# Fourth quarter of a pass: the order in which SyncE issues V's reads and writes and the read of projected rows

## The reference

```python
def _L0_ffn_ref(x, Wq, Wk, Wv, Ws, Wd, Wo):      # 16 heads, 8 experts, 2 chosen
    q = jnp.einsum('btc,hdc->bhtd', x, Wq)
    k = jnp.einsum('btc,hdc->bhtd', x, Wk)
    gate_v = jnp.einsum('btc,hec->bthe', x, Ws)
    w, sel = jax.lax.top_k(gate_v, K)
    mix_v = jnp.einsum('bthk,bthke->bthe', sigmoid(w), one_hot(sel))
    proj_v = jnp.einsum('btc,edc->bted', x, Wv)
    v = jnp.einsum('bthe,bted->bhtd', mix_v, proj_v)
    probs = softmax(einsum('bhid,bhjd->bhij', q * scale, k))
    attn = jnp.einsum('bhij,bhjd->bihd', probs, v)
    mask_o = ...                                  # top 2 of x @ Wd
    return jnp.einsum('bthe,bthd,efd->bthf', mask_o, attn, Wo).sum(axis=2)
...
x = x + 0.5 * _L0_ffn_ref(_layernorm(x), ...)
x = x + _L0_attn_ref(_layernorm(x), ...)
x = x + 0.5 * _L0_ffn_ref(_layernorm(x), ...)
```

## Time and profile before

| | |
|---|---|
| timed, median of 3 | 2392.2 us |
| the profiled execution's own time | 2388.17 us |
| its span, first to last instruction | 2386.4 us |
| TensorE clock granted | 0.998 of full speed |
| TensorE busy (matmul) | 2293.9 us, 96% |
| VectorE, ScalarE, GpSimd busy | 86%, 82%, 49% |
| DMA | 388 MB, mean 163 GB/s, queues 55% busy |

### The profile page before, as it was taken

The page is one execution under the profiler, slowest core; times in us unless marked ns, Lnnn a source line. Parts: engine busy times, 40 slices in busy tenths (PEclk is TensorE's granted clock), DMA queues, the critical chain, the costliest instruction groups (busy, mean ns, idle before and its releaser), DMA issues.

```text
span 2386.4 us, 120494 instructions
## 1 busy us (share of the span) xinstructions
PE 2293.9 (96%) x49920; PEld 2148.7 (90%) x49920; DVE 2060.7 (86%) x3755; ACT 1950.4 (82%) x6053; POOL 1161.0 (49%) x1190
## 2 busy tenths in 40 slices
PE   3999999999999999999999999999999999999997
PEld 3899898999999999999999999999999999999897
DVE  5888888989889898888989888888888888898884
ACT  2888787888888888888888888888888888888885
POOL 3445555455455454454454454454454454554431
PEclk9999999999999999999999999999999999999999
DMA  4555555655555555556556556556556555556553
GB/s 122 160 171 154 147 161 149 171 164 169 163 164 170 167 168 168 161 164 174 162 166 173 162 164 178 163 164 173 166 165 175 162 168 165 169 163 172 161 166 103
DMA packets 660701, 388.23 MB, mean 163 GB/s; under 512 B 232512, under 2 KB 585664, under 8 KB 660160
## 3 DMA queue, kind: packets, MB, share of 16 engines
q1 hardware_dynamic: 659728, 379.67, 55.0%
q10 hardware_dynamic: 432, 0.85, 0.1%
HBM read 191.64 MB, written 188.74 MB: 159 GB/s over the span
## 4 chain that ended last, share of the span: by engine, by line
PE 86%; ACT 6%; issue 4%; DVE 2%; POOL 1%; DMA 0%; SPq 0%; ACTq 0%; DVEq 0%; POOLq 0%
PE psT L477 19%; PE psS L432 15%; PE psT L494 8%; PE psT L496 6%; PE psT L495 6%; PE psS L524 6%; PE psT L524 6%; PE psT L445 6%; PE psT L489 5%; PE psT L459 5%; ACT PB L812 5%; ACT PJ L853 1%; DVE NMAX L693 1%; PE psT L603 1%; PE psT L530 1%
## 5 line engine op out<-in xcount | busy, mean ns | idle before, releaser
L812 ACT ACTIVATE PB<-psS,NMAX 128x256 f32<-128x256 f32 x2048 | 943.5, 488 | 101.4 <-DVE NMAX L693 101.4
L477 PE MATMUL psT<-V,PT 128*64 128x64 f32 x16384 | 544.3, 224 | 22.9 <-issue 22.2
L477 PEld LDWEIGHTS psT<-V,PT 128*64 128x64 f32 x16384 | 505.3, 138 | 51.7 <-issue 26.5
L812 ACT ACTIVATION_READ_ACCUMULATOR PB<-psS,NMAX 128x1 f32 x2048 | 452.8, 221 | 0.0
L761 DVE TENSOR_TENSOR QK<-psT,QK 128x512 fp32r<-128x512 f32 x512 | 349.0, 688 | 119.0 <-ACT QK L820 112.4
L432 PE MATMUL psS<-QK 64*128 64x256 f32 x6144 | 442.8, 288 | 3.1 <-DVE PT L765 2.6
L820 ACT ACTIVATE QK<-psT 128x512 fp32r<-128x512 f32 x512 | 307.3, 602 | 164.8 <-PE psT L496 141.0
L432 PEld LDWEIGHTS psS<-QK 64*128 64x128 f32 x6144 | 393.5, 187 | 8.3 <-issue 4.7
L693 DVE TENSOR_REDUCE NMAX<-psS 128x2 f32<-128x512 f32 x512 | 329.6, 685 | 51.5 <-PE psS L432 48.1
L927 POOL TENSOR_TENSOR BT<-MT,diagv 128x1024 f32<-128x1024 f32 x128 | 304.5, 2379 | 110.4 <-DMA MT<-MIXd 106.3
L933 POOL TENSOR_TENSOR MB<-MASKT,diago 128x1024 f32<-128x1024 f32 x128 | 250.2, 1956 | 144.3 <-DVE GM L770 116.4
(11 more groups left out here) (121 smaller groups left out, 4777.9 us busy)
## 6 DMA issues: line engine op xcount, KB each, us to landing
Vd<-VM SPq DMA_DIRECT2D x512, 128.0 KB, 2.3
V<-Vd SPq DMA_DIRECT2D x512, 128.0 KB, 3.1
AOd<-AO SPq DMA_DIRECT2D x256, 256.0 KB, 2.7
AR<-AOd SPq DMA_DIRECT2D x256, 256.0 KB, 4.1
PJd<-PJ SPq DMA_DIRECT2D x64, 512.0 KB, 2.8
PR<-PJd SPq DMA_DIRECT2D x256, 128.0 KB, 2.5
MIXd<-MIX SPq DMA_DIRECT2D x64, 128.0 KB, 2.3
MT<-MIXd SPq DMA_DIRECT2D x64, 128.0 KB, 3.3
```

The costliest lines, as they stand in the source:

```text
L477: last = eng.matmul(M[64 * u:64 * u + 64, (t * NT + it) * DH:(t * NT + it + 1) * DH], PT[:, t, jt, cols], V[:, pm % 2, 4 * r + t, jt, :], ...
L812: eng.activation(PB[:, ab, j, it, :], psS[:, ab, j, it, :], ACT.Exp, bias=NMAX[:, ab, j, it:it + 1], accum_out=SUM[:, p % 2, it, 4 * r + t ...
```

## The change

In the fourth quarter (r = 3) SP's order was: read V's first half, read PR, write V's second half, write AO. It becomes: write V's second half, wait for the quarter's product (`product` of n - 1), read V's first half, write AO, read PR. The write of AO stands ahead of the read of PR in the program of every quarter, but PR is read in the fourth alone, so the order changes only there. What TensorE, VectorE, ScalarE and GpSimd run is the same.

```diff
                 if r == 3 and runs(p + 1):
+                    store_values(p + 1, 1)
+                    wait_full(eng, "product", n - 1)
                     load_values(p + 1, 0)
+                if works(n - 1):
+                    m = n - 1
+                    wait_freed(eng, "product", m)
+                    if m >= 8:
+                        eng.wait_ge(s_ar, 16 * PARTS * (m // 4 - 1))
+                    eng.dma_start(AOd[m // 4 % 2]...[:, m % 4, :], AO[:, m % 2, :]).then_inc(s_aow[m % 2], 16)
                 if r == 3 and runs(p + 2):
                     q = p + 2
                     eng.wait_ge(s_pjw, 16 * (q + 1))
...
                         eng.dma_start(PR[:, own, :], stored[:, own, :]).then_inc(s_pr, 16)
-                if r == 3 and runs(p + 1):
-                    store_values(p + 1, 1)
-                if works(n - 1):
...
```

More of the change, by code:

```diff
@@ L375, in sync_program @@
                 if r == 3 and runs(p + 1):
+                    store_values(p + 1, 1)
+                    wait_full(eng, "product", n - 1)
                     load_values(p + 1, 0)
+                if works(n - 1):
[3 more added lines that the diff above has]
+                        eng.wait_ge(s_ar, 16 * PARTS * (m // 4 - 1))
+                    eng.dma_start(AOd[m // 4 % 2].rearrange("(p r x) -> p r x", p=P, r=4)[:, m % 4, :], AO[:, m % 2, :]).then_inc(s_aow[m % 2], 16)
                 if r == 3 and runs(p + 2):
```

## The result

| | before | changed |
|---|---|---|
| timed, median of 4 | 2394.65 us (2389.46 to 2398.71) | 2496.11 us (2486.87 to 2503.9) |
| ratio, with its 95% interval | | 1.0428 [1.0392, 1.0464] |
| the profiled execution and its span | 2388.17, 2386.4 us | 2503.9, 2502.1 us |
| granted clock of TensorE, mean | 0.998 | 0.986 |

The changed kernel is 4.3% slower, about 101 us. The prediction was 2378 us, with 2400 us as its upper end; the 2392.2 us from which it started is the median of the first three of the four runs of the kernel before. This is the page of the changed kernel; the first row answers to rows 1. The last row is the share of the final chain by engine.

What follows compares the result with a forecast made beforehand. TensorE, its matmuls busy 96% of the span, was taken as the bound, with late instruction fetches leaving it idle. -18 + 4 = -14 us from 2392.2 gave 2378 us; range 2368 to 2383 (also given as 2381), outer 2364 to 2400.

Steps and rivals of the forecast that it cites:

- The gain: Fourth quarter's product (L477): instruction fetch no longer late once V's first read leaves the quarter's start; 18 us, bounds 0 and 22.
- The fourth quarter's break: TensorE's idle after the 42nd of 64 product matmuls, every fourth pass, 13 times; 1.10 us idle in pass 31.
- 13 x 1.3: Thirteen breaks in fourth-quarter products, 1.3 us each, taken as 17 us of the gain.
- The write first: Fourth quarter: write of V's second half issued 0.9 us earlier; V's second read no longer waits for its landing.
- the new wait: Fourth quarter: SP reaches the wait for the product at 6.7 us, after its end at 4.94; costs nothing.
- V's second read: Next pass: V's second half read from 5.1 us, there at 10.8, needed at 11.24 or 11.68; priced at 4 us.
- The slower rival: First product of every pass (L477) waits for V's second half: 36 us less 18, 2410 us; chance 0.13.
- Behind that read stand MT, the masks and AR, all 3 to 5 us later: Reads behind V's second read in SP's queue come 3 to 5 us later; costed at nothing.
- a new one of values or expand: Sign in TensorE's waits: the prediction is wrong if a new wait of values or expand appears.
- 2 to 3 us are absorbed: GpSimd's idle before the second MB takes up 2 to 3 us of MT's lateness, before the values of r = 2.
- The bound of 54 us: Upper bound on V's second read: 60 x 0.9 us if it came 1.4 us later than worked out in every pass.
- its own covers: Spare time before the pass's first product needs V's second half: from 5.3 us to about 0.5 us.

Runs made afterwards that it cites:

- the shifted blocks: Kernel before with 16 more transposes of TensorE (32 instructions) once at the start: 2401.3 us, one run.
- AR alone late: Kernel before with one wait added, so the read of AR waits for TensorE's product of the second quarter: 2477.7 us, 1.0322.
- MT alone late: Kernel before with the read of MT moved behind the read of MASKT: 2446.7 us, 1.0207.
- both: Kernel before with MT read behind MASKT and AR's read waiting for the second quarter's product: 2499.6 us, 1.0409.
- the last runs: BT and MB each cut in two: MT behind MASKT 2426.6 us, changed kernel 2515.1, kernel before 2392.5, V's first read on ScalarE 2407.6.

## Why the prediction was wrong

- **The gain: right in place, somewhat too large.** The fourth quarter's break was a late block (shown by the shifted blocks), and it went with V's read, but for four pieces of 0.3 to 0.6 us. The odd passes' fourth quarters gained 0.43 us, all of it in those with number 3 modulo 4, which went from 9.82 to 8.98 us. That is 10 to 14 us in all against 18: 13 x 1.3 took a whole break for the gain of each.
- **The write first, the new wait: right.** On average the write starts at 4.72 us, as forecast, and V's read at 7.1 (6.8 forecast), with the product long done.
- **V's second read: right.** It began 5.0 us into the pass (5.1 forecast), and TensorE never waited for it. The slower rival had the right cause, SP's line pushed back, and the wrong victim.
- **The failed step** is "Behind that read stand MT, the masks and AR, all 3 to 5 us later" with "I cost these at nothing". The 3 to 5 us were right (4.4, 4.2 and 4.3 us), the nothing was about 101 us net and, with the gain of 10 to 14 us added back, about 113. Its own sign "a new one of values or expand" came true: 13.6 us of "issue" at `expand`. It checked each of these transfers against the time at which its data are wanted, and on that count it was right: TensorE's only wait for AR is one of 8.0 us at the program's end, as before, and its waits for AXN, MB and ST are 9 us. It didn't ask what each transfer and each product does to its new neighbours. AR's four reads of 256 KB, moved to the end of the second and the start of the third quarter, did there what V's read had done in the fourth, to a denser quarter; its own argument for the gain, applied to AR, would have given the loss. And "2 to 3 us are absorbed" was true for TensorE's waits for GpSimd, but F and EQ on VectorE took 59 us longer beside the moved products, and MT late by itself costs 50 us.
- **Two slips in its numbers, on which nothing hangs.** The bound of 54 us for a V 1.4 us later is 60 x 0.9, but by its own covers that is 0.96 us in even and 0.52 us in odd passes, 44 us. And the forecast's range ends once at 2381 and once at 2383 us.
- **The sizes.** AR alone late is +3.2%, MT alone late +2.1%, both +4.1%, the change +4.3%: 77, 50, 98 and 102 us of about 2396. The first two do not add up to the third; that one hides part of the other would explain it. A ledger of passes 10 to 59 of the changed kernel, whose total is 1906 - 1803 = 103 us: "issue" of TensorE +55.6 in third, +10.5 in second and -9.7 in fourth quarters, +9 for AXN, MB and ST, 3 for smaller waits. The other 34 us are TensorE busy for longer with the same matmuls. It was busy for 38.5 us at half clock, which by my estimate makes 19 of them; the other 15 are open.
- **Open.** How much of the loss in the changed kernel is the blocks' and how much VectorE's, as the two are not additive; that the first hides the second fits the last runs, and none shows it. Why a block comes later when the queues are busy (its packet standing behind others, or asked for late) was not tried. How much the low clock adds is an estimate from the trace, and no run isolates it.

## What to carry to other kernels

A change of order in one queue moves everything behind it. For each thing moved, look not only at when its data are wanted, but at what runs beside it at the new time: the DMA queues when the densest instruction stretch needs its next block, and VectorE's two-input instructions when GpSimd starts a long one. Idle time for "issue" that comes back every few turns at the same instruction may be a late block: adding a few instructions once at the start moves it if so. And if a gain is made by a quiet stretch of the queues, the traffic has gone somewhere, so find its new place first.

## What the runs showed of the hardware

- An instruction block that was late cost 1.1 us with queue q1 at 39.3%, and 3.85 us at a DMA share of 0.89. The Trainium skill (Runtime: NRT & Kernel Launch, section Instruction fetch mechanics) calls the crossing mostly hidden; in the changed kernel 49 us at two block boundaries of one line were not.
- Ten idle pieces of TensorE of 1.9 to 3.9 us in passes 10 to 59 of the changed kernel went with a stretch at half clock (0.50, 1.2 GHz) of 3.4 or 6.8 us; in the kernel before there was neither. A late block can be paid for twice.
- GpSimd's product of 2.0 us made a VectorE instruction of 0.69 us with two inputs in SBUF last up to 2.5 us. Two GpSimd instructions of half the length cost the kernel before nothing (0.9984 [0.9969, 0.9999]) and gave back 20 us where the two collide.
- A single issue of SyncE is sometimes held: in passes 9 to 59 of the kernel before 200 of 1731 took over 0.85 us, 169 of them while an instruction packet of q8 was under way, which holds of 354 of all.
